# First layer's attention: the mask of two head groups added by VectorE instead of TensorE

## The reference

```python
def _L0_xattn_ref(q, k, v, mask, wq, wk, wv, wo, bo):
    # q: layernorm(x), k and v: the context; 16 heads of 16 columns
    ...
    scores = jnp.einsum('nqha,nkha->nhqk', qh, kh)
    scores = jnp.where(mask == 0, jnp.float32(-10000000000.0), scores)
    attn = jax.nn.softmax(scores / math.sqrt(HEAD_DIM), axis=-1)
    out = jnp.einsum('nhqk,nkha->nqha', attn, vh).reshape(N, Lq, D_MODEL)
    return out @ wo + bo
x = x + jnp.tanh(g_xattn[0]) * _L0_xattn_ref(_layernorm(x, axis=-1), ctx_1024, ctx_1024, mask, wq, wk, wv, wo, bo)
```

## Time and profile before

| | us |
|---|---|
| median of 3 runs | 1793.32 |
| lowest and highest of them | 1789.34, 1793.98 |
| the profiled execution | 1796.88 |
| its span, first to last instruction | 1795.2 |
| of it VectorE's first score reduction of batch 1 to that of batch 15, 14 batches | 156.79 |

### The profile page before, as it was taken

The page is one execution under the profiler, slowest core; times in us unless marked ns, Lnnn a source line. Parts: engine busy times, 40 slices in busy tenths (PEclk is TensorE's granted clock), DMA queues, the critical chain, the costliest instruction groups (busy, mean ns, idle before and its releaser), DMA issues. The chain is left out here.

```text
span 1795.2 us, 32731 instructions
## 1 busy us (share of the span) xinstructions
PE 1370.8 (76%) x10700; PEld 1157.7 (64%) x10709; DVE 975.7 (54%) x2389; ACT 686.4 (38%) x1370; POOL 361.9 (20%) x452
## 2 busy tenths in 40 slices
PE   4999657749599993999999989999999951102554
PEld 3777535649599982788888878799999840102232
DVE  3777654627512215555555547423223736988786
ACT  2555443510244431333333333355554252302454
POOL 1000000001122210222222222366665300001000
PEclk9999967869599996999999988799999986556787
DMA  3000020770211106111111010122223324020001
GB/s 95 19 18 13 11 76 1 231 218 1 76 40 38 38 21 210 45 45 44 48 47 51 8 58 26 42 91 92 92 90 109 141 62 109 9 56 1 1 0 47
DMA packets 96891, 108.63 MB, mean 61 GB/s; under 512 B 27888, under 2 KB 83952, under 8 KB 96496
## 3 DMA queue, kind: packets, MB, share of 16 engines
q1 hardware_dynamic: 83168, 77.77, 14.4%
q0 software_dynamic: 9984, 27.28, 4.9%
q10 hardware_dynamic: 3664, 2.63, 0.5%
HBM read 85.55 MB, written 20.97 MB: 59 GB/s over the span
## 5 line engine op out<-in xcount | busy, mean ns | idle before, releaser
L3474 PEld LDWEIGHTS L2f_bank<-L2f_xT,L2f_w_tile 128*128 128x128 f32 x1280 | 156.1, 193 | 7.5 <-ACT L2f_xT L3534 3.5
L3474 PE MATMUL L2f_bank<-L2f_xT,L2f_w_tile 128*128 128x128 f32 x1280 | 156.9, 276 | 3.0 <-ACT L2f_xT L3534 3.0
L759 POOL TENSOR_TENSOR L2x_probs<-L2x_probs,L2x_inv_sum 128x512 f32<-128x512 f32 x64 | 65.2, 1040 | 289.4 <-DVE L2x_inv_sum L1026 289.4
L3583 DVE TENSOR_TENSOR L2f_hT<-L2f_gate_h,L2f_bank 128x256 f32<-128x256 f32 x80 | 33.7, 421 | 151.9 <-ACT L2f_gate_h L3541 151.9
L3528 ACT COPY L2f_w_tile<-L2f_w_up 128x1024 f32 x80 | 83.7, 1046 | 34.8 <-issue 34.8
L3474 PEld LDWEIGHTS L1f_bank<-L1f_xT,L1f_w_tile 128*128 128x128 f32 x768 | 90.7, 194 | 1.1
L3474 PE MATMUL L1f_bank<-L1f_xT,L1f_w_tile 128*128 128x128 f32 x768 | 90.9, 277 | 0.0
L3399 POOL DMA_INDIRECT L2f_y_rows<-L2f_xn,L2f_put_row x80 | 79.0, 987 | 56.2 <-DVE L2f_xn L3599 52.7
L3391 POOL DMA_INDIRECT L2f_rows<-L2f_x_rows,L2f_take_row x80 | 77.8, 972 | 45.3 <-DVE L2f_take_row L3374 21.6
L1008 DVE TENSOR_REDUCE L2x_top<-L2x_bank 128x4 f32<-128x512 f32 x64 | 43.9, 686 | 78.8 <-PE L2x_bank L828 78.8
L3491 PE MATMUL L1f_bank<-L1f_w_down,L1f_hT 128*128 x384 | 86.7, 379 | 0.0
(11 more groups left out here) (649 smaller groups left out, 3340.5 us busy)
## 6 DMA issues: line engine op xcount, KB each, us to landing
L1f_w_up<-in_L_ffn_w SPq DMA_DIRECT2D x16, 512.0 KB, 9.6
L1f_w_down<-in_L_ffn_w SPq DMA_DIRECT2D x16, 512.0 KB, 9.0
L2f_got<-L2f_y_rows SPq DMA_DIRECT2D x16, 512.0 KB, 4.1
L2f_w_up<-in_L_ffn_gate_w SPq DMA_DIRECT2D x16, 256.0 KB, 2.8
L2f_w_up<-in_L_ffn_up_w SPq DMA_DIRECT2D x16, 256.0 KB, 2.9
L2f_w_down<-in_L_ffn_down_w SPq DMA_DIRECT2D x16, 256.0 KB, 3.6
x<-in_x SPq DMA_DIRECT2D x4, 512.0 KB, 7.6
L0x_ctx<-in_ctx SPq DMA_DIRECT2D x16, 128.0 KB, 2.1
```

The lines of the kernel that those rows point to most:

```text
L759: nc.gpsimd.tensor_tensor(probs[c][:, :, :], probs[c][:, :, :], inv_sum[:, c, :][:, :, None].to_broadcast([P, 4, P]), ALU.mult).then_inc(s ...
L3474: x = nc.tensor.matmul(products(j, m), w_tile[j][:, at:at + P], xT[j][:, k * P:(k + 1) * P], start=(k == 0), stop=(k == KT - 1))
L3583: nc.vector.tensor_tensor(hT[j][:, 0:F], gate_h[j][:, 0:F], bank[2 + j][:, F:2 * F], ALU.mult).then_inc(q["h"], 1)
```

## The change

For groups 1 and 3 TensorE's mask product goes away, and their score products no longer accumulate onto the mask: each starts and stops its own quarter of the bank. TensorE waits for a new semaphore, `masked`, before it writes those two banks, in place of `shifted`. VectorE's `shift` for these two groups begins with a new instruction: a scalar_tensor_tensor that reads the mask (16 bits, SBUF, repeated for the four heads), multiplies it by 1, adds the scores (PSUM) and writes the sum to `shifted[1]` (32 bits, SBUF). The reduction waits for it and reads the sum from there, and the subtraction works in place. Groups 0 and 2 stay as they were.

```diff
@@ scores, under block.tensor
                 for i in range(4):
 
-                    after(pe, s["shifted"], b * 4 + (i - 3))
-                    nc.tensor.matmul(score_bank[i][:, :].rearrange("p (h k) -> p h k", h=4), mask_diag[:, :],
-                                     mask_add[j][:, None, :].to_broadcast([P, 4, P]), start=True, stop=False)
+                    if i % 2 == 1:
+                        after(pe, s["masked"], (b - 1) * 2 + (i + 1) // 2)
+                    else:
+                        after(pe, s["shifted"], b * 4 + (i - 3))
+                        nc.tensor.matmul(score_bank[i][:, :].rearrange("p (h k) -> p h k", h=4), mask_diag[:, :],
+                                         mask_add[j][:, None, :].to_broadcast([P, 4, P]), start=True, stop=False)
...
                             last = nc.tensor.matmul(score_bank[i][:, at:at + P], qT[j][rows, odd, t, :],
-                                                    kT[j][rows, t, :], start=False, stop=(at == 3 * P))
+                                                    kT[j][rows, t, :], start=(i % 2 == 1),
+                                                    stop=(i % 2 == 1 or at == 3 * P))
@@ shift, under block.vector
-            def shift(b, i):
+            def shift(j, b, i):
                 src = score_bank[i][:, :].rearrange("p (h k) -> p h k", h=4)
 
                 dve.wait_ge(s["scores"], b * 4 + (i + 1))
+                if i % 2 == 1:
+                    after(dve, s["exped"], b * 4 + (i - 1))
+                    nc.vector.scalar_tensor_tensor(shifted[1][:, :, :],
+                                                   mask_add[j][:, None, :].to_broadcast([P, 4, P]), L0_MASK["diag"],
+                                                   src, ALU.mult, ALU.add).then_inc(s["masked"], 1)
+                    src = shifted[1][:, :, :]
+                    dve.wait_ge(s["masked"], b * 2 + (i + 1) // 2)
                 nc.vector.tensor_reduce(top[:, i % 2, :], src, AX.X, ALU.max).then_inc(s["maxed"], 1)
```

More of the change, by code:

```diff
@@ L309, in narrow_attention @@
         s = core.sems_in(tag, NORM_SEMS + [
-            "w_q", "w_k", "w_v", "w_o", "diag", "cleared", "parity", "ctx_in0", "ctx_in1", "mask_in0", "mask_in1",
+            "w_q", "w_k", "w_v", "w_o", "diag", "masked", "cleared", "parity", "ctx_in0", "ctx_in1", "mask_in0", "mask_in1",
             "mask_add", "xn", "filled", "evicted", "scores", "maxed", "shifted", "exped", "pT", "pT_out", "pv",
@@ L596, in body @@
                     norm(j, b + 2)
-                shift(b, 0)
-                shift(b, 1)
-                shift(b, 2)
+                shift(j, b, 0)
+                shift(j, b, 1)
+                shift(j, b, 2)
                 if not first:
                     take_heads(1 - j, b - 1)
-                shift(b, 3)
+                shift(j, b, 3)
                 if not two_left(b):
```

## The result

The changed kernel takes **1809.07 us** (median of four runs, 1805.88 to 1813.43) against 1793.29 us of the kernel before (four runs, 1789.34 to 1793.98). The ratio is 1.0094, with a 95% interval of 1.0067 to 1.0122: slower, and inside the predicted range of 1800 to 1811. The profiled execution took 1813.43 us, its span is 1811.7 us, 16.5 us more than before's 1795.2.

A forecast was written before the change was run, and what follows sets the result against it. The prediction took a ring through VectorE's row as the bound: additions 23.0 us less 3.4 covered, 19.6, less 7.9 from removed mask products, gave +11.7 us on the 1793.32 us median: 1805.0 us, range 1800 to 1811.

The forecast's parts named there:

- The ring through VectorE's row: First layer's attention: VectorE's row, exp, transposes, masks and scores each wait for the one before, 11.2 us a batch.
- Additions, 1.44 us a batch: VectorE's row: two mask additions, each making it 0.72 us longer; 23.0 us over 16 batches.
- Room, 0.19 us in batches 1 to 13: Lateness of group 3's exp behind a ScalarE copy covers 2.5 us; with 0.9 in batch 0, 3.4 us covered.
- Mask products, 0.48 us a border: TensorE between batches: two fewer mask products at 0.24 us each give back 7.2 us over 15 borders.
- Ahead of batch 0, 0.7 us: Before the first reduction: two fewer mask products at 0.36 us each give back 0.7 us.
- Moved reads at nothing: Reductions and subtractions of groups 1 and 3 reading SBUF instead of PSUM: at most 1.1 us saved, taken as nothing.
- the rival of cheaper SBUF reads: VectorE's SBUF reads are cheaper: 1.1 us less by the rows, 4.1 us by the Trainium skill's rule; 5%.
- New waits at nothing: Group 3's addition waiting for group 1's exp, and TensorE's two new waits, are for things long past: no cost.
- The clock falls: Rival: TensorE's longer waits drop one batch in four to 1.2 GHz, 31 us more, 1836 us; 4%.
- A granted clock under 0.95 in the stage: Sign, in TensorE's granted clock during the first layer's attention, that the forecast is wrong.
- The delay goes through to the end: Behind the stage's barrier nothing is loaded ahead, so the whole +11.7 us reaches the program's end.
- a missing gain on TensorE: Rival: waits and register instructions fill the removed products' place, losing half to all of 7.9 us, 1809 to 1813 us; 10%.

The follow-up runs named there:

- the halves: The change's two parts run apart: VectorE's additions with all mask products kept, 1812.84 us, and two mask products taken out with no additions, 1787.38 us.
- additions alone: Changed kernel with all four mask products put back on TensorE, so groups 1 and 3 get the mask twice: 1812.84 us.
- the same kernel with a delay behind it: Kernel before with 56 filler products behind its last projection, only delaying the barrier: 1803.10 us.
- the run again: The changed kernel once more, unaltered, with a second profile: 1810.07 us.
- fillers to the end: Changed kernel with unread products in TensorE's waits before group 3's transposes in every batch, more in the last batch and ahead of the last projection: 1806.61 us.
- the one above: The change on top of a version with one maximum per group of four heads and no subtractions, group 3 handled behind the reciprocal: 1781.85 us.
- products removed: Kernel before without the mask products of groups 1 and 3 and with no additions in their place: 1787.38 us.

## Why the prediction was right, and where it was off

- **What bounds the stage**: right. The ring through VectorE's row, the exp, the transposes, the masks and the scores sets the period, as the halves showed: lengthening the row costs its length less the room, shortening the mask products gives their length.
- **Additions, 1.44 us a batch**: right. 8.35 us instead of 6.90 from first reduction to last subtraction, 1.45.
- **Room, 0.19 us in batches 1 to 13**: right. The period grew by 1.25 us instead of 1.44 with the additions alone. In batch 0 less was covered than forecast: with the 0.43 us that TensorE gave back there, the +0.29 in the table mean 0.72 us for VectorE's part, where 0.5 was forecast.
- **Mask products, 0.48 us a border**: mis-sized. 0.43, because 0.10 us of the 0.96 don't depend on their number. Over the batches it is most of the 0.6 us between +9.24 and +9.86 to +9.91.
- **Ahead of batch 0, 0.7 us**: not seen. In the first profile the two products there run at 1.2 GHz, 30.47 to 31.46, and from the first of them to the first reduction it is 2.84 us against 2.64 before. The 0.36 us a product weren't its price either: with the additions alone four products take 0.96 us at the same place (31.84 to 32.80, granted clock 1.00). The 1.73 us in the table come from ahead of the products (30.47 against 32.40), and this start lies between 33.3 and 35.7 us in the profiles of this study, whatever the kernel.
- **Moved reads at nothing, and the rival of cheaper SBUF reads**: nothing, right. See below.
- **New waits at nothing**: right. No idle time is put down to them in VectorE's row, and the period needs no further term.
- **The clock falls**: held too low, and in the wrong place. The middle batches stay at 1.00 with waits of 1.57 us on TensorE, and no batch in four fell. But batches 13 and 14 together had 0.93 and the part behind them 0.66, which cost 4.7 us; in the second profile batch 14 kept its clock, the last part had 0.72, and it cost 2.2 us. The prediction read 52% busy at 0.97 as evidence that a loosely filled stretch keeps its clock; it was one draw, and the same kernel with a delay behind it fell there too. "A granted clock under 0.95 in the stage" was named as a sign that would make it wrong, and it came, at the end of the stage.
- **The delay goes through to the end**: right between the profiles of before and after (+0.09 us), but behind the barrier 5 us come and go with the next stage's clock, which the range didn't name.

The sum of 11.7 us, made from the first reduction of batch 0 to the barrier, was 12.4; with the clock held at 2.4 GHz by fillers it measures 13.4. Measured between the medians the change costs 15.8 us, the run again 16.0, the fillers to the end 12.5. The median fell 4 us above the forecast; the clock at the end of the stage, 4.7 and 2.2 us in the two profiles, is the one cause for it that the profiles show. That the range held the result is therefore in part luck: its upper 6 us stood for a missing gain on TensorE and for longer additions, and neither came; the clock used them.

## What to carry to other kernels

Before moving work from a busy engine to a less busy one, look for the row that stands shoulder to shoulder between two waits: here the engine with 93% of the stage covered was the one that waited. The same change cost 0.83 us a batch when the receiving engine's row was on the ring, gave next to nothing (0.02 us) when the additions stood behind the reciprocal, and gave 0.42 us when it had room ahead of it. So the room has to lie ahead of the instruction that the others wait for, not anywhere in the batch. Judge such a change by its period in the steady loop, and look at the clock of the loosely filled batches at the ends apart.

## What the runs showed of the hardware

- A maximum reduction of 128x512 fp32 takes the same from SBUF as from PSUM; the 17 ns of the earlier trace rows don't show in it. Groups of VectorE's instructions in the kernel after (busy us, mean ns):

```profile
L577 DVE TENSOR_REDUCE L0x_top<-L0x_bank 128x4 f32<-128x512 f32 x32 | 22.0, 688 | 33.3 <-PE L0x_bank L414 33.3
L577 DVE TENSOR_REDUCE L0x_top<-L0x_shifted 128x4 f32<-128x512 f32 x32 | 22.0, 686 | 1.1
```

The rule of the Trainium skill, "VectorE: DVE Perf Modes", section on the TRN2 errata, of 62 cycles between the two sources isn't followed here.

- Four products of 128x512 in 16 bits took 0.96 us to the next kind of product, two 0.53: 0.215 us each and 0.10 us once.
- The granted clock stayed at 1.00 through twelve batches with a wait of 1.57 us on TensorE in each, filled or not. From the last batch's first reduction to the barrier TensorE's same work ran at 0.97, 0.72 and 0.66 in the profile of before and the two of the changed kernel: one reading of such a stretch doesn't tell what the next execution gets.
- After a wait TensorE's next instructions followed less closely here: mask products 0.43 us after the start of four transposes that didn't wait, 0.49 or some 0.7 us, in turns from batch to batch, after ones that did (137.85 to 138.34 in the kernel after, 113.48 to 114.17 in the one above, 140.11 to 140.84 with products removed).
